# Recurrence read-out: the skip term moved from VectorE into diagonal matrix products, and the gate by z onto VectorE alone

## The reference, cut to what matters

```
h_t   = tanh(h_{t-1} + A^T xconv_t)          state of 16 numbers a batch
y     = C h + Dp * xconv                     Dp: one factor for each channel
x     = x + ga * (W_out^T (y * z) + b_out)
```

## Time and profile before

| | us |
|---|---|
| median of 3 runs | 2018.14 (2017.99 to 2021.9) |
| the profiled execution, its own time | 2019.34 |
| its span in the trace | 2017.6 |
| TensorE busy, of the span | 1769.4 (88%) |
| VectorE busy, of the span | 1467.7 (73%) |
| GpSimd busy, of the span | 644.0 (32%) |
| read-out, from its first product to the end of its last addition | 127.45 to 154.67 |

### The profile page before, as it was taken

One profiled execution on the slowest core, in us unless ns is written; L12 is line 12 of the kernel. 1 busy time (PEld: TensorE's weight loads), 2 busy tenths in 40 slices (PEclk: granted clock), 3 DMA queues, 4 the chain that ended last, 5 costly groups with the idle time before them and its releaser, 6 DMA issues. The chain is left out here.

```text
span 2017.6 us, 33658 instructions
## 1 busy us (share of the span) xinstructions
PE 1769.4 (88%) x12569; PEld 649.5 (32%) x12569; DVE 1467.7 (73%) x3109; ACT 1096.3 (54%) x1385; POOL 644.0 (32%) x776
## 2 busy tenths in 40 slices
PE   6547889999999999999599888888888888889898
PEld 3115433333333333333333342111211211112465
DVE  5875766666666666663535689999999999994743
ACT  4402244454455445455323248888887878887432
POOL 0031445544554555442133203302402410001153
PEclk8868999999999999999899989999999999999798
DMA  4000000000000000000030201211221211220114
GB/s 135 0 0 1 1 3 33 24 32 24 23 24 23 23 23 34 24 31 26 20 113 37 78 13 70 84 44 44 75 84 46 86 65 60 85 78 9 64 33 145
DMA packets 56270, 91.69 MB, mean 45 GB/s; under 512 B 21652, under 2 KB 30164, under 8 KB 55980
## 3 DMA queue, kind: packets, MB, share of 16 engines
q1 hardware_dynamic: 54540, 85.86, 12.3%
q0 software_dynamic: 1280, 2.62, 0.4%
q10 hardware_dynamic: 288, 1.05, 0.2%
HBM read 46.15 MB, written 38.51 MB: 42 GB/s over the span
## 5 line engine op out<-in xcount | busy, mean ns | idle before, releaser
L1811 DVE TENSOR_REDUCE h_m_half<-h_ps_max 128x1 f32<-128x512 f32 x1024 | 635.9, 682 | 31.7 <-PE h_ps_max L1418 28.9
L1667 ACT ACTIVATE h_P<-h_ps_st 128x1024 f32<-128x1024 f32 x512 | 497.8, 1023 | 86.4 <-PE h_ps_st L1434 83.7
L887 PE MATMUL l_ps_st<-l_Q,l_K 64*128 64x512 f32 (+3 forms) x1536 | 310.3, 498 | 3.6 <-DMA l_Q<-l_m_row 1.3
L1047 ACT ACTIVATE l_P<-l_ps_st 128x1024 f32<-128x1024 f32 (+3 forms) x256 | 207.6, 834 | 191.2 <-PE l_ps_st L887 190.7
L1138 DVE CUSTOM_DVE_ANT_0 l_masked<-l_ps_t,l_mask 128x384 bf16<-128x384 f32 (+3 forms) x512 | 229.2, 485 | 62.7 <-PE l_ps_t L841 62.5
L1444 PE MATMUL h_ps_o<-h_P,h_V 128*9 128x512 f32 x2048 | 267.7, 595 | 0.7 <-ACT h_P L1667 0.5
L1418 PE MATMUL h_ps_max<-h_K,h_Q 48*128 48x512 bf16 x1024 | 201.2, 390 | 66.8 <-DVE h_m_half L1811 64.7
L1141 DVE TENSOR_REDUCE l_m_half<-l_ps_t 128x1 f32<-128x512 f32 x256 | 164.5, 685 | 70.0 <-PE l_ps_t L841 68.6
L1434 PE MATMUL h_ps_st<-h_Q,h_K 51*128 51x512 bf16 x1024 | 167.3, 379 | 14.6 <-ACT h_P L1667 10.6
L1418 PEld LDWEIGHTS h_ps_max<-h_K,h_Q 48*128 48x128 bf16 x1024 | 49.3, 93 | 386.1 <-DVE h_m_half L1811 371.3
L1715 POOL CAST h_m_parts<-h_m_neg 128x16 bf16<-128x16 f32 x32 | 6.3, 196 | 517.3 <-DVE h_m_neg L1775 517.3
(11 more groups left out here) (456 smaller groups left out, 2386.2 us busy)
## 6 DMA issues: line engine op xcount, KB each, us to landing
sums<-l_o SPq DMA_DIRECT2D x15, 512.0 KB, 2.7
sums<-h_o SPq DMA_DIRECT2D x15, 512.0 KB, 2.6
h_K<-k_parts SPq DMA_DIRECT2D x32, 192.0 KB
h_Q<-q_parts SPq DMA_DIRECT2D x32, 192.0 KB
y_rows<-zero SPq DMA_DIRECT2D x8, 512.0 KB, 4.9
c_W<-c_W SPq DMA_DIRECT2D x32, 128.0 KB, 2.1
c_W<-in_W SPq DMA_DIRECT2D x16, 256.0 KB, 3.9
c_back<-y_rows SPq DMA_DIRECT2D x16, 256.0 KB, 5.6
```

Source lines behind the costliest of these rows:

```text
L887: last = pe.matmul(ps_st[x % 2][:, a, 0:w], K[n // NG % 2][rows, kt * 128:(kt + 1) * 128], Q[n % NQ][rows, c, p, q0 - c * CH:q0 - c * CH + ...
L1047: act.activation(P[e % PR][:, :, 0:w], ps_st[slot["s", n, i, p] % 2][:, :, 0:w], ACT.Exp, scale=0.125).then_inc(consumed, 1)
L1667: act.activation(P[e % PR][:, :, :], ps_st[x % 2][:, :, :], ACT.Exp, scale=1.0 / 12.0).then_inc(consumed, 1)
L1811: dve.tensor_reduce(m_half[:, half, 2 * p + a, qt:qt + 1], ps_max[:, t % NB, :], AX.X, ALU.max, negate=True)\
```

## The change

The skip term is no longer computed on VectorE. GpSimd writes, in the first stage, two 128 by 128 matrices with Dp on the diagonal. TensorE multiplies xconv by such a matrix into PSUM and leaves the accumulation open, and the product C h, of 32 rows, is added to it there. For the first part the diagonal products are issued in the first stage, behind the last `drive`; PSUM for them is therefore kept over both stages. VectorE then makes y * z from PSUM in one multiplication for every batch, and GpSimd has nothing left in the second stage. The waits go batch by batch: TensorE's list is, for part k and batch b, the diagonal product of part k + 1, the product C h of part k + 1, and the projection of part k. `added` and `out_ready` go by batch too.

```diff
+        Dp_diagonal = outer.enter_context(nc.sbuf_tensor("Dp_diagonal", [128, 2, 128], F32))
+        ps_kept = [outer.enter_context(nc.psum_tensor(f"ps_kept{i}", [128, T], F32)) for i in range(2)]
+        ps_y = [ps_kept[b // 2][:, (b % 2) * CH:(b % 2 + 1) * CH] for b in range(B)]
...
-            ps = [ctx.enter_context(nc.psum_tensor(f"ps_in{i}", [128, T], F32)) for i in range(3)]
+            ps = [ctx.enter_context(nc.psum_tensor("ps_in", [128, T], F32))] + ps_kept
...
                 pool.drain().then_inc(padded, 1)
+                for m in range(2):
+                    pool.tensor_scalar(Dp_diagonal[:, m, :], S.ident[:, :], S.vec("Dp", m), None, ALU.mult).then_inc(diagonal_set, 1)
...
                 drive(B - 1)
+                pe.wait_ge(diagonal_set, 2)
+                pe.wait_ge(evacuated, 4 * B)
+                for b in range(B):
+                    pe.matmul(ps_y[b], Dp_diagonal[:, 0, :], xconv[:, 0, batch(b, 0)], start=True, stop=False)
                 pe.wait_ge(judged, 2)
...
-            ORDER = (1, 0, 2, 3)
+            PARTS = [(c, m) for c in range(2) for m in range(2)]

             @block.tensor
             def _(pe):
-                def outputs(c, m):
-                    if c or m:
-                        pe.wait_ge(skipped, B * (2 * c + m))
+                def output(k, b):
+                    c, m = PARTS[k]
+                    if k:
+                        pe.wait_ge(gated, B * (k - 1) + b + 1)
+                        pe.matmul(ps_y[b], Dp_diagonal[:, m, :], xconv[:, m, batch(b, c)], start=True, stop=False)
+                    pe.matmul(ps_y[b], CT_sb[32 * b:32 * b + 32, m * 128:(m + 1) * 128],
+                              hs[32 * b:32 * b + 32, 1 + c * CH:1 + (c + 1) * CH], start=False, stop=True).then_inc(read, 1)
+
+                def project(k, b):
+                    c, m = PARTS[k]
+                    pe.wait_ge(gated, B * k + b + 1)
+                    if k == 2:
+                        pe.wait_ge(added, b + 1)
+                    last = pe.matmul(ps_o[b][:, :], Wout_sb[:, m, :], xconv[:, m, batch(b, c)], start=(m == 0), stop=(m == 1))
+                    if m:
+                        last.then_inc(out_ready, 1)
+
+                for b in range(B):
+                    output(0, b)
+                for k in range(4):
                     for b in range(B):
...
+                        if k < 3:
+                            output(k + 1, b)
+                        project(k, b)
...
-            @block.gpsimd
-            def _(pool):
-                for c in range(2):
-                    for m in range(2):
-                        for b in range(1, B):
-                            pool.wait_ge(skipped, B * (2 * c + m) + b)
-                            pool.tensor_tensor(xconv[:, m, batch(b, c)], xconv[:, m, batch(b, c)], sz[:, m, batch(b, c)],
-                                               ALU.mult).then_inc(gated, 1)

             @block.vector
             def _(dve):
...
+                def gate(k, b):
+                    c, m = PARTS[k]
+                    dve.wait_ge(read, B * k + b + 1)
+                    dve.tensor_tensor(xconv[:, m, batch(b, c)], ps_y[b], sz[:, m, batch(b, c)], ALU.mult).then_inc(gated, 1)
+
+                def add(c, b):
+                    dve.wait_ge(out_ready, B * c + b + 1)
+                    dve.scalar_tensor_tensor(out=S.xT[:, batch(b, c)], in0=ps_o[b][:, :], scalar=S.mod[:, 0, 2, b:b + 1],
+                                             in1=S.xT[:, batch(b, c)], op0=ALU.mult, op1=ALU.add).then_inc(added, 1)
+
+                for k in range(4):
+                    for b in range(B):
+                        gate(k, b)
+                        if k == 2:
+                            add(0, b)
+                for b in range(B):
+                    add(1, b)
```

More of the change, by code:

```diff
@@ L351, in recurrent @@
             judged, worst_turned = semaphore(nc, ctx, "newton_judged"), semaphore(nc, ctx, "newton_turned")
-            scaled = semaphore(nc, ctx, "ssm_scaled")
+            scaled, diagonal_set = semaphore(nc, ctx, "ssm_scaled"), semaphore(nc, ctx, "ssm_diagonal")
             block = ctx.enter_context(nc.Block())
@@ L485, in recurrent @@
         with stage(nc) as ctx:
-            ps_y = [ctx.enter_context(nc.psum_tensor(f"ps_y{b}", [128, CH], F32)) for b in range(B)]
             ps_o = [ctx.enter_context(nc.psum_tensor(f"ps_o{b}", [128, CH], F32)) for b in range(B)]
-            read, skipped, gated_first, gated, out_ready, added = [
-                semaphore(nc, ctx, f"ssm_{x}") for x in ("read", "skipped", "gated_first", "gated", "out", "added")]
+            read, gated, out_ready, added = [semaphore(nc, ctx, f"ssm_{x}") for x in ("read", "gated", "out", "added")]
@@ L490, in recurrent @@
             block = ctx.enter_context(nc.Block())
-            ORDER = (1, 0, 2, 3)
+            PARTS = [(c, m) for c in range(2) for m in range(2)]
             @block.tensor
             def _(pe):
-                def outputs(c, m):
-                    if c or m:
-                        pe.wait_ge(skipped, B * (2 * c + m))
-                    for b in range(B):
[L499 to L521, removed]
@@ L532, in _ @@
             @block.vector
             def _(dve):
[L534 to L551, removed]
@@ L552, in _ @@
-                skip(1, 1)
-                add(1)
+                def gate(k, b):
[6 more added lines that the diff above has]
+                                             in1=S.xT[:, batch(b, c)], op0=ALU.mult, op1=ALU.add).then_inc(added, 1)
```

## The result

The changed kernel takes 2042.47 us (median of 4 runs, 2038.99 to 2043.21) against 2019.55 us of the kernel before in the same comparison (4 runs, 2017.99 to 2021.9). The ratio is 1.0099, with a 95% interval of 1.0085 to 1.0113: 17 to 23 us slower. The medians themselves differ by 22.9 us, the upper end of that. The forecast was slower by 18.0 us, 2036.1 us, with a range up to 2039.5. Direction, place and unit were right, and 1.0089 as a ratio lies inside the interval; the time itself lies above the range. The profiled execution has a span of 2041.0 us, 23.4 more than before.

What follows compares the result with a forecast made beforehand. TensorE was taken to bound the read-out. Resumption at 130.31, 5.05 us cold, 32.92 of units, 3.44 of projections and 0.95 end gave 172.67 against 154.67: 18.0 us more, 2036.1 us, range 2031.0 to 2039.5.

Steps and rivals of the forecast that it cites:

- the clock term: Read-out start: clock stays at half for 5.05 us after TensorE resumes, bounds 3.3 and 7.1 us, worth -0.8 and +1.0 us.
- the resumption: Read-out after part 0: TensorE goes on at 130.31, 2.04 us earlier than before, the gain of the waits by batch.
- The second rival: Read-out: lone C h costs more, or clock stays low or falls again; +3.4 us, near 2039.5; chance 0.08.
- The bound: Read-out stage: TensorE is already the busiest engine, ahead of VectorE with 14.12 us.
- The unit of 2.96 us: Read-out: diagonal, C h and projection of one batch take 2.96 us at full clock; 12 such units.
- The third and fourth rivals: Read-out: lone C h overlaps its neighbours, +3.2 us, chance 0.04; or VectorE sets the pace, -7.7 us, chance 0.03.
- The first rival: Read-out: steps between product heights cost nothing, -4.5 us against the forecast, 2031.6 us; chance 0.10.
- What is hidden: Part-0 diagonals (3.4 us) and GpSimd writes lie under earlier work; VectorE's gates lie under TensorE's units.
- What follows the read-out: Later stages move back whole, with about 1.5 us of chance either way from clock dips.

Runs made afterwards that it cites:

- probe with lone products: Kernel before plus 12 products of 32 rows, all in one row group, in TensorE's Newton-round pause; no clock rise in 20.5 us.
- kernel without diagonals: Changed kernel without its sixteen diagonal products, the skip term left out of y; ratio 1.0148 to the kernel before, median 2050.66 us.
- mixed probe: Kernel before plus 12 products ordered full, 32 rows, full, four times, in TensorE's Newton-round pause; clock rose after 6.6 us.
- second profile: Changed kernel run once more, nothing altered; ratio 1.0085 to the kernel before, read-out 46.53 us, clock rise 7.54 us after TensorE resumed.
- grouped: Changed kernel with TensorE's list reordered per part: four diagonals, four C h side by side, four projections; ratio 1.0032 to the kernel before, read-out 33.73 us.
- the probes: Four kernels, each the kernel before plus full, lone 32-row, mixed or four-side-by-side products in the Newton rounds; clock rise after 5.45 us, never, 6.6, 3.2.
- kernel before, warmed: Kernel before plus twelve full products into dead PSUM ahead of its read-out; ratio 1.0000 to the kernel before, read-out 26.75 us.

## Why the prediction was wrong, and what in it held

The time, 2042.47 us, lies above the upper bound of 2039.5. By the profiled execution the span grew by 23.4 us in place of 18.0: 3.8 us of the 5.4 between them are the clock term, 0.14 the resumption, 0.1 the other terms of the read-out and 1.4 what follows it. On top of that the kernel before itself stood 1.4 us above the 2018.14 that the forecast was added to.

- **The clock. This term failed,** by its size and its bounds: "Before, it rose at 137.4, 5.05 us after TensorE resumed and then stayed busy. I take 5.05 us again", with at most 7.1. The runs gave 12.85 and 7.54 us. The step carried a duration from a stretch of mostly full products over to one in which a third of the passes are lone 32-row ones. The probe with lone products (no rise in 20.5 us) and the kernel without diagonals (none in 48 us, with half the passes lone) show that the clock need not rise at all under such work. How much later it rises under the changed kernel's mix, two full to one lone, is known from three executions only, 12.85, 7.54 and 6.6 us (the mixed probe), and chance is a good part of the spread; the read-out of before gave 4.1 to 5.3 us in five. The second rival held this case ("the clock stays low or falls again under alternating work") but priced only a rise at 137.4, and a clock that never rose. With 12.85 in the sum it ends at 176.5, and 176.72 was measured; with the 7.54 of the second profile the same sum is only 1.2 us over the forecast. So the size of the miss owes something to the execution, its direction does not.
- **The bound.** Right. TensorE was already the busiest engine of the stage, and work moved onto it came back as time; the order of the list, with what it did to the clock, cost more than the added work: 13 to 15 us (grouped) against the 6.5 left.
- **The unit of 2.96 us.** Right to 0.005 us, in the changed kernel and by its parts: 2.57 us where no height changes, 8.13 us for a part where four C h stand side by side. The prediction had no lone 32-row product to read: its "one" with 0.53 us was the 64-row product of the earlier trace rows. The changed kernel has the 32-row one, and its first pass is 0.53 us too (149.56 to 150.09). The rule of the Trainium skill, "TensorE: Matmul & The Clock Gate", section "Why this matters for your kernels", that a single product of 32 rows takes the time of one of 128 rows, held: in the probes, at half clock and without steps, both stand 0.85 us apart. The third and fourth rivals, in which lone products hide or VectorE sets the pace, fell with the unit. The first rival, steps for nothing, fell too: they are 0.39 us a unit.
- **The resumption.** Predicted at 130.31, came at 130.45. That its 2.04 us are "the gain of the waits by batch" is only half of it: with the same waits in the kernel before TensorE resumed as early, 2.9 us after its first product, but the projections behind came no sooner. That the changed kernel keeps the gain because VectorE has one instruction a batch there and its list goes on batch by batch is argued, not tested.
- **What is hidden.** The part-0 diagonals, the two GpSimd writes and the gates cost nothing that shows, as forecast.
- **What follows the read-out.** It was costed as a shift with 1.5 us of chance either way. It was 1.4 us longer in the first profile and 2.0 in the second. Chance is larger than was taken: in the seven traces in which the read-out is that of before or nearly so, it took 1862.1 to 1866.2 us; in the seven of the changed kernel and its variants, 1864.0 to 1867.9. Whether the change adds to it is not shown. The kernel before, too, stood at 2019.55, 2022.0 and 2020.2 us in the three comparisons.

## What to carry to other kernels

Products of few rows are cheap only side by side: before a wait is made finer or work is added between them, count what the array does by the distance of starts, one for a group and one for each that will stand alone. Where a stretch starts at half clock, the time until the clock rises depends on what is issued, and an interleaving that looks busy can hold it down; put the full products first and the small ones together (read-out 13 to 15 us shorter here), or pad the small one to full height if it must stand alone (6 to 9 us shorter here). Less work on TensorE is not less time if the work taken away was what brought the clock up.

## What the runs showed of the hardware

TensorE can be busy without a gap for 51.2 us at 1.2 GHz. In the pause of the Newton rounds 20.5 us of lone 32-row products brought no rise to 2.4 GHz, nor did 48 us in the read-out in which they alternated with full ones; full products (5.45 us) and four 32-row ones side by side (3.2 us) did. The Trainium skill, "TensorE: Matmul & The Clock Gate", "What's actually happening", says that the warm-up is a budget of time and not a number of matmuls, and that the clock follows how busy TensorE has been. The traces disagree with the first of these for products that use 32 of the 128 rows, and "busy" in the second cannot be the busy share that the profile prints.

Once up, the clock stayed up over 42 us of the changed kernel's mix, in which TensorE waited once for 0.7 us. In the kernel before, warmed, it fell 3.1 us after the start of the read-out, 2.0 us into a wait of 2.8 us.

Each step between heights stood 0.52 in place of 0.43 us at full clock, and the first pass behind it 0.53; where all products had 128 rows both were gone (2.57 us a unit). The Trainium skill, "TensorEngine Tiling (Array Packing)", "Key Properties", says that a change of tiling mode drains the engine; the distances fit that, though a drain itself is not seen in a trace.
